# One gather in 32 moved from GpSimd to the sync queue, row by row, in a graph attention kernel

## What is computed

```python
def hgt_conv(x, src, dst, ntype, etype, Wk, Wq, Wv, Wa, pri, att, msg, skip):
    k, q, v = (typed_linear(x, ntype, W).reshape(n, H, HD) for W in (Wk, Wq, Wv))
    kw = typed_linear_heads(k[src], etype, att)
    a = sum(kw * q[dst], -1) * pri[:, etype].T / sqrt(HD)
    w = softmax of a over the edges of one destination
    m = typed_linear_heads(v[src], etype, msg) * w[:, :, None]
    h = segment_sum(m, dst, n).reshape(n, D)
    alpha = sigmoid(skip)[ntype][:, None]
    return typed_linear(h, ntype, Wa) * alpha + x * (1 - alpha)
for l in range(5): h = hgt_conv(h, ...)
return layernorm(x + h)
```

## Time and profile before

| | us |
|---|---|
| median of three runs | 6741.87 (6736.51 to 6746.9) |
| the profiled execution | 6739.41 |
| its span, first to last instruction | 6737.6 |

### The profile page before, as it was taken

One profiled execution on the slowest core, in us unless ns is written; L12 is line 12 of the kernel. 1 busy time (PEld: TensorE's weight loads), 2 busy tenths in 40 slices (PEclk: granted clock), 3 DMA queues, 4 the chain that ended last, 5 costly groups with the idle time before them and its releaser, 6 DMA issues.

```text
span 6737.6 us, 151874 instructions
## 1 busy us (share of the span) xinstructions
PE 4691.4 (70%) x33354; PEld 4001.1 (59%) x33355; DVE 5048.9 (75%) x14709; ACT 4031.0 (60%) x10574; POOL 4269.9 (63%) x4670
## 2 busy tenths in 40 slices
PE   2976666688666666976666669676666786666664
PEld 1766565566665555765656657665555676555652
DVE  6677777777777777777777777777777778777776
ACT  0466666644766666456666654666666447666661
POOL 0277777724777776267777743777777347777761
PEclk8988878889878887988888779878888898878877
DMA  1633333334333333533333335333333343333331
GB/s 45 255 102 103 104 103 103 103 150 173 101 103 103 104 103 87 211 124 104 103 104 102 103 101 220 102 103 103 104 103 103 141 179 100 103 103 103 103 93 38
DMA packets 273850, 774.98 MB, mean 115 GB/s; under 512 B 88031, under 2 KB 104516, under 8 KB 272708
## 3 DMA queue, kind: packets, MB, share of 16 engines
q0 software_dynamic: 199680, 545.53, 27.5%
q1 hardware_dynamic: 73668, 224.51, 8.6%
HBM read 573.87 MB, written 195.88 MB: 114 GB/s over the span
## 4 chain that ended last, share of the span: by engine, by line
PE 30%; issue 19%; DVEq 19%; DVE 16%; POOL 10%; DMA 4%; ACT 2%; ACTq 1%; POOLq 0%; SPq 0%
POOL rows L462 10%; DVEq L1266 6%; DVEq L1256 5%; PE ps L572 5%; PE ps L749 4%; PE ps L733 4%; PE ps L754 3%; PE ps L596 3%; DMA rows<-table,idx_now 3%; PE ps L583 2%; DVEq L244 2%; PE ps L566 2%; PE ps L748 2%; DVE prod L1250 1%; DVE wmsg L1232 1%
## 5 line engine op out<-in xcount | busy, mean ns | idle before, releaser
L462 POOL DMA_INDIRECT rows<-table,idx_now x4160 | 4036.4, 970 | 1395.6 <-issue 1157.7
L847 ACT ACTIVATE prod<-iota_n,dloc 128x128 bf16<-128x128 f32 x6240 | 1983.5, 389 | 19.6
L748 PE MATMUL ps<-zeros,identb 128*128 128x132 bf16 x2080 | 522.1, 251 | 1543.9 <-DVE wmsg L1232 1267.0
L733 PE MATMUL ps<-qn,ohT 128*128 x8320 | 1444.2, 327 | 76.5 <-issue 56.2
L733 PEld LDWEIGHTS ps<-qn,ohT 128*128 128x128 f32 x8320 | 1266.6, 232 | 154.2 <-issue 135.6
L748 PEld LDWEIGHTS ps<-zeros,identb 128*128 128x128 bf16 x2080 | 227.6, 109 | 1717.3 <-issue 1624.4
L852 ACT ACTIVATE ohf<-prod,ones 128x512 f32<-128x512 bf16 x1040 | 750.7, 722 | 769.8 <-PE ps L754 691.3
L749 PE MATMUL ps<-wmsg,ohf 128*128 128x132 f32 x4160 | 1138.2, 363 | 0.0
L754 PE MATMUL ps<-wmsg,ohf 128*128 128x132 f32 x4160 | 992.0, 328 | 0.0
L1228 DVE TENSOR_TENSOR wmsg<-rows,weight 128x512 f32<-128x512 f32 x1040 | 720.9, 693 | 346.6 <-issue 314.4
L1250 DVE TENSOR_TENSOR prod<-ps,rows 128x512 f32<-128x512 f32 x1040 | 714.8, 687 | 291.1 <-DMA rows<-table,idx_now 162.3
(11 more groups left out here) (166 smaller groups left out, 5516.2 us busy)
## 6 DMA issues: line engine op xcount, KB each, us to landing
table<-rows SPq DMA_DIRECT2D x245, 768.0 KB, 3.3
rows<-table,idx_now POOLq DMA_INDIRECT x4160
rows<-in_node_type SPq DMA_DIRECT2D x5, 2613.0 KB, 10.6
out<-h SPq DMA_DIRECT2D x1, 3072.0 KB
rows<-in_node_type SPq DMA_DIRECT2D x5, 512.0 KB, 4.4
wk<-in_L_gnn_Wk SPq DMA_DIRECT2D x20, 48.0 KB
wq<-in_L_gnn_Wq SPq DMA_DIRECT2D x20, 48.0 KB
wv<-in_L_gnn_Wv SPq DMA_DIRECT2D x20, 48.0 KB
```

The lines of the kernel that those rows point to most:

```text
L462: pool.indirect_dma_start(out=rows[:, slot, j, :], out_offset=None, in_=table, in_offset=bass.IndirectOffsetOnAxis(ap=idx_now[:, half, c:c ...
L733: last = pe.matmul(ps[:, 2 + b, j * P:(j + 1) * P], ohT[:, b, j, :], qn[:, at(ts[j]), :].rearrange("p a c -> p (a c)"), start=True, stop=True)
L748: pe.matmul(bank[:, AW:2 * AW], identb[:], zeros[:], start=True, stop=True)
L847: act.activation(squares[:, turn % 2, j * P:(j + 1) * P], iota_n[:], ACT.Square, bias=dloc[:, at(4 * q + j)], scale=-1.0)
```

## The change

In blocks 1 to 25 of each layer, the last step of the block (the fourth of the eighth quad) is no longer gathered by GpSimd, which issues 31 gathers a block. In block 0 nothing changes, except that this one gather counts a semaphore of its own.

The sync queue fetches that step's rows instead. In the preparation VectorE makes `row_of`, the row numbers of those steps times 256, a column for each block. For each block the sync queue copies a column of it into one partition (`index_row`), loads the numbers into registers, four at a time, and issues 128 DMAs of one row each, from the table at the register's address to one partition of `stage`, which has two buffers (`gather_rows`). Sixteen rows share a semaphore. When all have landed and the ring slot is free, one more DMA copies them from the stage to the ring (`to_ring`), and VectorE waits for that one (`s_side`) beside the three gathers of the quad's slot. The first sixteen rows of the next block are issued ahead of `to_ring`, the others behind it. Block 1 is fetched at the start of the stage, before the next layer's weights are loaded.

```diff
+    table_flat = table.rearrange("(o n) c -> o (n c)", o=1)
...
+            def index_row(n, b):
+
+                sp.dma_start(idx_row[0:1, b, :], row_of[:, at(n)]).then_inc(s_irow[b], 16)
+
+            def gather_rows(l, n, b, turns, first_group, end_group):
+
+                if first_group == 0:
+                    hold(sp, s_irow[b], l * (BLOCKS // 2 * 16) + turns * 16 + 16)
+                for g in range(first_group, end_group):
+                    for i in range(g * GROUP, (g + 1) * GROUP, 4):
+                        _, at_rows = nc.values_load_multi_w_load_instructions(
+                            idx_row[0:1, b, i:i + 4], engines=[mybir.EngineType.SP], min_val=0,
+                            max_val=(TILES * P * ET - 1) * ROW,
+                            skip_runtime_bounds_check_because="an edge's row is 6 times its source node plus its type")
+                        for j in range(4):
+                            sp.dma_start(stage[i + j:i + j + 1, b, :], table_flat[:, at(at_rows[j], ROW)]
+                                         ).then_inc(s_row[b][g], 16)
+
+            def to_ring(l, n, b, turns):
+
+                for g in range(GROUPS):
+                    hold(sp, s_row[b][g], l * (RUNS[b] * 16 * GROUP) + turns * (16 * GROUP) + 16 * GROUP)
+                slot = b * BQ + BQ - 1
+                hold(sp, s_wm, l * QUADS + n * BQ + (BQ - RING + 1))
+                sp.dma_start(rows[:, slot, 3, :], stage[:, b, :]).then_inc(s_side, 16)
+
+            def ring_filled(l, n):
+
+                hold(sp, s_side, l * ((BLOCKS - 1) * 16) + n * 16)
+
             def edges_(l):
                 wa_load(l)
                 hold(sp, s_wa, l * (16 * R4) + 16 * R4)
+                index_row(1, 1)
+                gather_rows(l, 1, 1, 0, 0, GROUPS)
                 if not isinstance(l, int):
                     hold(sp, s_qn, l * TILES + TILES)
                     weights(l + 1)
                     hold(sp, s_w, l * WN + 2 * WN)
+                index_row(2, 0)
+                with sp.Fori(0, BLOCKS // 2 - 1) as it:
+                    gather_rows(l, it * 2 + 2, 0, it, 0, 1)
+                    to_ring(l, it * 2 + 1, 1, it)
+                    index_row(it * 2 + 3, 1)
+                    gather_rows(l, it * 2 + 2, 0, it, 1, GROUPS)
+                    ring_filled(l, it * 2 + 1)
+                    gather_rows(l, it * 2 + 3, 1, it + 1, 0, 1)
+                    to_ring(l, it * 2 + 2, 0, it)
+                    index_row(it * 2 + 4, 0)
+                    gather_rows(l, it * 2 + 3, 1, it + 1, 1, GROUPS)
+                    ring_filled(l, it * 2 + 2)
+                to_ring(l, BLOCKS - 1, 1, BLOCKS // 2 - 1)
+                ring_filled(l, BLOCKS - 1)
...
-                    for j in range(4):
+                    by_pool = 3 if slot % BQ == BQ - 1 and not is_first(n) else 4
+                    for j in range(by_pool):
                         c = 4 * (slot % BQ) + j
                         pool.indirect_dma_start(
                             out=rows[:, slot, j, :], out_offset=None, in_=table,
                             in_offset=bass.IndirectOffsetOnAxis(ap=idx_now[:, half, c:c + 1], axis=0)
-                        ).then_inc(s_gath[slot], 16)
+                        ).then_inc(s_seventh if slot == BQ - 1 and j == 3 else s_gath[slot], 16)
...
+            dve.memset(row_of[:], 0)
+            dve.drain()
+            dve.tensor_scalar(row_of[:, 0:BLOCKS].rearrange("p (n c) -> p n c", c=1),
+                              idx[:, 0:BLOCKS * BS].rearrange("p (n s) -> p n s", s=BS)[:, :, BS - 1:BS], float(ROW),
+                              None, ALU.mult)
...
-                        dve.wait_ge(s_gath[slot], (l * (QUADS // RING) + use) * 64 + 64)
+                        if slot % BQ < BQ - 1:
+                            dve.wait_ge(s_gath[slot], (l * (QUADS // RING) + use) * 64 + 64)
+                        else:
+                            dve.wait_ge(s_gath[slot], (l * (QUADS // RING) + use) * 48 + 48)
+                            if is_first(n):
+                                dve.wait_ge(s_seventh, l * 16 + 16)
+                            else:
+                                dve.wait_ge(s_side, l * ((BLOCKS - 1) * 16) + n * 16)
```

More of the change, by code:

```diff
@@ L44 @@
 SP_ = 4 * QUADS
+GROUPS = 8
+GROUP = P // GROUPS
 BS, BQ = 32, 8
 BLOCKS = QUADS // BQ
+RUNS = (BLOCKS // 2 - 1, BLOCKS // 2)
 assert BLOCKS * BQ == QUADS and BS * H == P and BS == 4 * BQ
@@ L88, in gnn @@
         tile_of = sb("tile_of", [1, SP_], I32)
+        row_of = sb("row_of", [P, BLOCKS + 1], I32)
         idx_now = sb("idx_now", [P, 2, BS], I32)
@@ L124, in gnn @@
         wmsg = sb("wmsg", [P, 2, 4, AW])
+        stage = sb("stage", [P, 2, ROW])
+        idx_row = sb("idx_row", [1, 2, P], I32)
         score = sb("score", [P, 2, P])
@@ L196, in gnn @@
         s_h = sem("h_updated")
+        s_side = sem("rows_of_queue_in_ring")
+        s_seventh = sem("last_step_of_first_block_gathered")
+        s_irow = [sem(f"index_row_loaded{i}") for i in range(2)]
+        s_row = [[sem(f"rows_staged{i}_{g}") for g in range(GROUPS)] for i in range(2)]
         s_gath = [sem(f"gathered{i}") for i in range(RING)]
@@ L388, in edges_ @@
                     hold(sp, s_w, l * WN + 2 * WN)
+                index_row(2, 0)
[12 more added lines that the diff above has]
+                ring_filled(l, BLOCKS - 1)
+                hold(sp, s_irow[0], l * (BLOCKS // 2 * 16) + BLOCKS // 2 * 16)
             def output_(l):
```

## The result

| | before | after |
|---|---|---|
| median, us | 6742.2 (6736.51 to 6746.9) | 10944.7 (10940.61 to 10949.88) |
| span of the profiled execution, us | 6737.6 | 10944.5 |

The ratio of after to before is 1.6234, 95% interval 1.6206 to 1.6262. The change makes the kernel 4200 us slower. The prediction had the direction and the mechanism, but 8940 us, and its range ended at 10400.

The account below looks back on a forecast made before the run. GpSimd's gather issue was taken to bound the kernel, then the sync queue at 59.3 us a block (55.3 for rows): 439 us a layer, 2196 in five, added to 6741.9 gives 8940 us; range 7450 to 10400.

Parts of the forecast that it names:

- What bounds the kernel now: Edge stage: GpSimd's issue, one gather every 1.272 us, 40.7 us a block, with VectorE close behind at about 38.5.
- what the change takes away: GpSimd in the edge stage: 24 gathers a layer, 30.5 us, or 153 us in five layers.
- rival 1: The sync queue keeps up, a row taking 0.31 us or less, and GpSimd's 31 gathers bound: 6589 us, chance 0.08.
- What is late next: Edge stage: the strictly serial sync queue sets the period, 439 us more a layer, 2196 in five.
- 24 P - 984: Edge stage: us lost per layer, P being the sync queue's time for one block; 439 us at the forecast 59.3.
- the price of a row: Sync queue, one row: 0.34 us for the DMA with its address plus 0.092 for its load share, 0.432 together.
- the rest of a block: Sync queue, besides the rows: 11 waits 2 us, two more DMAs 1 us, the loop's jump 1 us.
- three cases: A row's DMA with its address: 0.34 us with a MOVE alone; with both instructions, 0.31 if shortened, 0.42 if not.
- partial absorption: Sync queue: register work ahead of a DMA partly comes back as a shorter DMA; a row's beat 0.267 if all absorbed.
- the unseen one: Sync queue's register load of four, priced from TensorE's and VectorE's at 0.37 us with its gap, 0.092 a row.
- Rival 2: One-row transfers queue on one DMA engine, each waiting out the previous landing of 1.8 us: about 29400 us, chance 0.02.
- What would show it: Signs in the changed profile: rows at 0.4 to 0.5 us, VectorE waiting some 20 us a block, edge stages near 1555.

Follow-up runs that it names:

- experiment 2: The changed kernel without the one-row DMAs and their loads; the sync queue only copies a stage of zeros to the ring once a block: 6647.5 us.
- experiment 6: The kernel before, with short stretches of register loads and one-row DMAs added to the idle sync queue, three kernels: 6748.5, 6746.7 and 6752.2 us.
- experiment 5: The changed kernel with one register load of sixteen numbers for sixteen rows in place of four loads of four: 9684.5 us.
- experiment 3: The changed kernel with one register load of four for each sixteen rows, its four registers used four times each: 8250.8 us.
- experiment 1: The changed kernel with its 128 one-row DMAs a block at fixed addresses, without register loads or register addresses: 6639.1 us, ratio 0.985.

## Why the prediction was wrong

*What bounds the kernel now.* Right for the beat of GpSimd, 1.272 us a gather and no wait. Wrong for what stands behind it. I took VectorE's own pace, 38.5 us a block, from two early blocks. In the kernel that only copies (experiment 2) it is about 40 in the middle of the stage, where it is the bound. The row for that was there: in the earlier trace rows VectorE waits 22.4 us for gathered rows in 950, which is 0.96 a block, and 40.7 - 0.96 = 39.8. So what the change takes away is 92 us and not 153; in the forecast of 8940 this term was hidden, and it did no harm there, but rival 1 with its 6589 us could not have come true.

*What is late next.* Right in the mechanism, and lucky in its constant. The serial queue is the period; 24 P - 984 gave 10942 for 10944.7, 8260 for 8250.8, 8767 for 8736.4 (P = 57.9), and with P = 65.7 for the loads of sixteen 9703 for 9684.5. But the formula lets the first copy of a layer wait for quad 0 alone, at 395 us, with 9 us to spare for the weights. In the changed kernel block 1's rows went on until 381.8, and the landings of the weights and of the index row then stood in the chain that ended last, ahead of the copy (start, duration, what; the copy from the timeline):

```profile
393.15 2.78 DMA priw<-in_L_gnn_rel_pri
396.02 2.56 DMA idx_row<-row_of
...
408.46 0.51 SPq L417 DMA_DIRECT2D rows<-stage  x1
```

That is 11 to 14 us too late in each of the four layers that load weights. The other way went three things: the last copy of a layer follows its neighbour by 65.2 us, 10.8 less than P and not 7; from it to the last product it is 2.0 us, where the formula has 4.5; and in the last layer P is 75.6. From its first product to its last the edge stage is 847, 845, 847, 841 and 820 us longer than before, 4200 in all, five times the 840 of the formula.

*The step that failed is the price of a row*, 0.432 us where 71.77 / 128 = 0.561 was measured, in both of its terms. The range failed with it, as the register load had no upper bound of its own:

| term of the sum, us | forecast | upper bound | measured |
|---|---|---|---|
| a DMA with its address | 0.34 | 0.433 | 0.41 |
| a load of four, with its gap | 0.37 | 0.37 | 0.61 |
| 128 rows | 55.3 | 67.2 | 71.8 |
| the rest of a block | 4.0 | 4.7 | 4.2 |
| P | 59.3 | 71.9 | 76.0 |

The DMA. I had three cases, and chose the one with a MOVE alone. Each row got both instructions (16000 ALU_OPs, 16000 MOVEs). The hope for partial absorption, taken from wk's DMAs (431 ns alone, 317 behind register work), did not hold for one row: 0.25 us alone (the 32 fixed rows of experiment 6 at 0.30 with their gap) and 0.225 behind both. With the loads taken off, (71.77 - 32 x 0.61) / 128 = 0.41 is left, inside the bounds, and the unabsorbed value 0.42 was in the text. 128 x 0.07 = 9 us a block.

The load. This was "the unseen one", and I gave it one value and no bounds of its own: TensorE's and VectorE's 332 and 343 ns are rows of sequencers that issue no DMA. The sync queue's load is 0.30 behind another load, but 0.56 behind a DMA, and in this kernel they stand behind DMAs. 32 x 0.24 = 7.7 us a block, 24 x 7.7 x 5 = 920 us in all. A bound from above would have widened the range to hold the time: with the highest bound for the row and 0.61 for the load, P = 128 x 0.433 + 32 x 0.61 + 4.7 = 79.6.

The Trainium skill's floor of about 600 ns for `tensor_load` (DMA: Bandwidth & Descriptors, Latency and other measured facts), which I set aside since the trace did not agree, is near what this place has, 0.556 in the median and 0.60 with its gap. It is no floor: the same load took 0.30 behind another one, on the same queue, and 0.33 on two others. The measurements decide; what the page has right is a case, that of a load between DMAs.

*Rivals.* Rival 1 (the queue keeps up) needed a row at 0.31 us and is false at 0.56; at fixed addresses (0.294) the queue does keep up, and 6639 us was measured, not rival 1's 6589. Rival 2 (the rows queue on a DMA engine) is false, by the same run.

*What would show it.* Rows at 0.4 to 0.5 us with their load: 0.56. VectorE's wait once a block at the eighth quad, "some 20 us": 33 to 39. Edge stages 440 us longer (1555 against 1115): 820 to 847. All in kind, none in size. The projections are nearly unchanged, as forecast: 278 us from a layer's last product to the next one's first in the first layer before, 280 now.

## What to carry to other kernels

A DMA issued per row costs its sequencer, on the sync queue here, 0.22 us of issue and 0.34 more in address work, gaps and its share of a load; 128 of them were 72 us against the 1.27 of one indirect DMA on GpSimd. So such work belongs on an idle queue only in the amount that fits the period, which is found by dividing, before building: here half of it did, and that half was worth 63 us. Price an instruction that the trace does not show on its engine with two bounds, also when two other engines agree on it, because its neighbours there may differ. And before counting a relief of the bound engine in full, look at how long the next one waits for it: that wait, 0.96 us a block here or 115 us in all, bounded the 92 us that could be had better than the 153 counted.

## What the runs showed of the hardware that I had not expected

- A register load of four values on the sync queue takes 0.30 us behind another load, 0.46 as the first one after a wait of 1 or 40 us, and 0.56 right behind a DMA (experiment 6). One load of sixteen values (1.23 us) was cheaper than four of four between the DMAs, 9684.5 us against 10944.7 (experiment 5); several loads in a row ahead of their DMAs should be cheaper too, which no kernel here tried.
- Register work ahead of a one-row DMA is hardly absorbed: the DMA's 0.25 us becomes 0.225, while 0.06 us of instructions and some 0.06 of gaps are added.
- A register used again as an address needs no second register operation (4000 for 16000 rows in experiment 3).
- A stream of one-row DMAs of 1 KB every 0.29 us, beside gathers, slowed nothing that could be measured: 6639 us with them, 6647 without. A row travels as one packet of 1 KB and a small one, about 0.06 us of a DMA engine's time (experiment 1).
